# Second and third attention: float32r halves of two heads side by side on TensorE, queries in halves, maxima ahead

## The reference

```python
def _L1_attn_ref(x, wq, bq, wk, bk, wv, bv):
    xq = (x @ wq + bq).reshape(B, S, 32, 16)
    xk = (x @ wk + bk).reshape(B, S, 8, 16)
    xv = (x @ wv + bv).reshape(B, S, 8, 16)
    q, k = _rope(xq, cos, sin), _rope(xk, cos, sin)
    k, v = repeat(k, 4), repeat(xv, 4)
    probs = softmax(einsum('bqhd,bkhd->bhqk', q, k) / sqrt(16))
    return einsum('bhqk,bkhd->bqhd', probs, v)
def _L2_attn_ref(x, w_q, w_k, w_v, w_o):
    q, k, v = proj(w_q), proj(w_k), proj(w_v)
    attn = softmax(einsum('bqhd,bkhd->bhqk', q, k) / sqrt(16))
    return einsum('bhqk,bkhd->bqhd', attn, v) @ w_o.T
```

## Time and profile before

| | us |
|---|---|
| median of 3 runs (2819.14 to 2826.78) | 2824.91 |
| profiled execution | 2823.69 |
| its span, first to last instruction | 2821.9 |

### The profile page before, as it was taken

The page is one execution under the profiler, slowest core; times in us unless marked ns, Lnnn a source line. Parts: engine busy times, 40 slices in busy tenths (PEclk is TensorE's granted clock), DMA queues, the critical chain, the costliest instruction groups (busy, mean ns, idle before and its releaser), DMA issues. The chain is left out here.

```text
span 2821.9 us, 36229 instructions
## 1 busy us (share of the span) xinstructions
PE 2376.8 (84%) x12928; PEld 1296.4 (46%) x12928; DVE 1475.5 (52%) x2491; ACT 1247.3 (44%) x1599; POOL 640.1 (23%) x478
## 2 busy tenths in 40 slices
PE   4979999999997776599999957599989996999657
PEld 3657777777776532223333223233333333444434
DVE  3564545554542545678777554287778723112253
ACT  3536565555653322065656632136655662000331
POOL 1645656565651124000000022100000001001021
PEclk8989999999998887699999968799999998999778
DMA  4861111111103111100000002401021003000001
GB/s 112 247 186 42 41 56 52 56 45 56 52 27 106 42 51 53 49 14 16 15 15 15 1 15 75 113 14 24 23 44 25 1 16 120 0 0 0 17 4 53
DMA packets 76898, 133.98 MB, mean 47 GB/s; under 512 B 29848, under 2 KB 39320, under 8 KB 74480
## 3 DMA queue, kind: packets, MB, share of 16 engines
q1 hardware_dynamic: 76784, 132.35, 15.7%
HBM read 94.44 MB, written 37.62 MB: 47 GB/s over the span
## 5 line engine op out<-in xcount | busy, mean ns | idle before, releaser
L2151 POOL TENSOR_TENSOR l0a_p_low<-yT,l0a_p_high 128x1024 fp32r<-128x1024 f32 (+7 forms) x256 | 386.1, 1536 | 281.9 <-ACT l0a_p_high L2179 281.9
L1432 DVE TENSOR_REDUCE l2a_mx<-ps 128x1 f32<-128x512 f32 x512 | 338.1, 689 | 125.6 <-PE ps L1273 124.2
L1432 DVE TENSOR_REDUCE l1a_mx<-ps 128x1 f32<-128x512 f32 x512 | 336.9, 688 | 112.2 <-PE ps L1273 110.3
L2212 DVE TENSOR_REDUCE l0a_mx<-ps 128x1 f32<-128x512 f32 (+3 forms) x384 | 203.5, 554 | 236.1 <-PE ps L2058 145.7
L1399 ACT ACTIVATE l2a_prob<-ps 128x1024 f32<-128x1024 f32 x256 | 250.5, 1019 | 131.3 <-PE ps L1312 93.7
L1399 ACT ACTIVATE l1a_prob<-ps 128x1024 f32<-128x1024 f32 x256 | 250.6, 1019 | 129.9 <-PE ps L1312 93.7
L173 POOL TENSOR_TENSOR applied<-prepared,neghalf 128x2 f32<-128x2 f32 x64 | 58.4, 913 | 900.0 <-DVE prepared L154 900.0
L1273 PE MATMUL ps<-l1a_k,l1a_q 96*128 96x512 bf16 x512 | 199.0, 398 | 64.6 <-DMA l1a_k<-l1a_k_parts 47.7
L2168 ACT ACTIVATE yT<-ps 128x1024 f32<-128x1024 f32 (+7 forms) x256 | 166.4, 650 | 186.9 <-PE ps L2080 122.9
L1273 PE MATMUL ps<-l2a_k,l2a_q 96*128 96x512 bf16 x512 | 192.0, 389 | 47.2 <-DMA l2a_k<-l2a_k_parts 34.4
L2179 ACT CAST l0a_p_high<-yT 128x1024 fp32r<-128x1024 f32 (+7 forms) x256 | 172.6, 674 | 7.1
(11 more groups left out here) (303 smaller groups left out, 4357.3 us busy)
## 6 DMA issues: line engine op xcount, KB each, us to landing
l0a_q<-l0a_q SPq DMA_DIRECT2D x32, 512.0 KB, 3.3
l0q_woh<-in_l0a_wo SPq DMA_DIRECT2D x16, 512.0 KB, 5.6
l0a_q<-f SPq DMA_DIRECT2D x32, 256.0 KB, 4.7
l0a_q<-l0q_q_pe SPq DMA_DIRECT2D x32, 256.0 KB, 3.6
l0a_recip_rows<-l0a_recip_row SPq DMA_DIRECT2D x32, 256.0 KB, 3.4
l0a_o<-l0a_o_pair SPq DMA_DIRECT2D x16, 512.0 KB, 2.8
yT<-l0a_o SPq DMA_DIRECT2D x16, 512.0 KB, 3.3
l0q_wqnT<-in_l0a_wqnT SPq DMA_DIRECT2D x16, 192.0 KB, 3.5
```

What stands on the lines that cost most here:

```text
L1432: nc.vector.tensor_reduce(mx[:, m // NT, m % NT, c:c + 1], MB[c], AX.X, ALU.max).then_inc((s_red0, s_red1)[c], 1)
L2151: nc.gpsimd.tensor_tensor(p_low[:, j % 4, P * j:T], prob[:, j % 4, P * j:T], p_high[:, j % 4, P * j:T], ALU.subtract).then_inc(s_pl, 1)
L2212: nc.vector.tensor_reduce(mx[:, qt, c:c + 1], bank(par, n)[:, 0:width], AX.X, ALU.max).then_inc(s_red, 1)
```

## The change

In `split_qk` each tile has two parts instead of three: ACT casts to float32r (`high`), DVE subtracts (`low`), and both are stored as 4-byte words in DRAM arrays of 32 rows.

In `attend` two heads lie side by side in the rows: rows 0 to 47 hold (high, low, high) of the one head's queries against (high, high, low) of its keys, rows 64 to 111 those of the other, and rows 48 and 112 the maxima against ones. One call therefore makes a pair of matmuls, one for each head, into two PSUM banks. A step is one pair of scores: two heads, 128 keys, 512 queries; a group has 32 steps in two halves of the queries. One pair of maxima is issued in each step, eight steps further ahead than one group, and the chunks use three banks in a ring, which a group's transposed maxima (now once per group) enter too. The products with the values are four matmuls of 512 queries, eight in a half, at the steps `PV_STEP`, read from `vext` without the copy to `vst`. `prob` has four slots of j. The loops of PE, ACT and DVE are written out.

```diff
-Q_RUNS = [(0, 3), (1, 2), (2, 1)]
-K_RUNS = [(0, 3), (0, 2), (0, 1)]
+STEPS = HALVES * NT * 2
+PAIRS_OF_MAX = 2 * NT * 2
+RING = 3
+MAX_ROW = 3 * HD
+AHEAD = 8
+TURN_STEP = STEPS - AHEAD + 2
+PV_STEP = (7, 8, 9, 10, 12, 14, 16, 18)
+OUT_STEP, TURN_OUT_STEP, FINISH_STEP = 19, 20, 21
...
-                    nc.scalar.copy(part[0:M, n % 2, 0, :], tile_of(n)).then_inc(s_part, 1)
-                    act.wait_ge(s_lo, 2 * n + 1)
-                    nc.scalar.copy(part[0:M, n % 2, 1, :], rest[0:M, n % 2, :]).then_inc(s_part, 1)
+                    wait_stored(act, n)
+                    nc.scalar.copy(high[0:M, n % 2, :], tile_of(n)).then_inc(s_high, 1)
...
-                    nc.vector.tensor_tensor(part[0:M, n % 2, 2, :], rest[0:M, n % 2, :], part[0:M, n % 2, 1, :],
-                                            ALU.subtract).then_inc(s_lo, 1)
+                    nc.vector.tensor_tensor(low[0:M, n % 2, :], tile_of(n), high[0:M, n % 2, :],
+                                            ALU.subtract).then_inc(s_low, 1)
...
+            def load(g):
+                s, slot = loaded[g % SLOTS][0], g % SLOTS
+                for hf in range(2):
+                    heads = slice(g * GROUP + hf, (g + 1) * GROUP, 2)
+                    sp.dma_start(q_bits[64 * hf:64 * hf + 2 * HD, slot, :, :], q_dram[:, heads, :]).then_inc(s, 16)
...
+            sp.wait_ge(s_one, b_one + 2)
+            for g in range(SLOTS):
+                load(g)
...
+            for hf in range(2):
+                nc.gpsimd.memset(k_bits[64 * hf + 32:64 * hf + 64, :, :, :], 1.0).then_inc(s_one, 1)
...
+            def max_pair(m):
...
+                for hf in range(2):
+                    wait_bank(pe, ("chunk", 2 * m + hf))
+                for hf in range(2):
+                    rows = slice(64 * hf, 64 * hf + MAX_ROW)
+                    mm = nc.tensor.matmul(bank(("chunk", 2 * m + hf)), q[rows, slot, p, qt * P:(qt + 1) * P],
+                                          k[rows, slot, p % KP, 512 * c:512 * c + 512], start=True, stop=True)
+                mm.then_inc(s_mm, 1)
...
+            def pv(g, half, j):
...
+                for hh in range(GROUP):
+                    mm = nc.tensor.matmul(O[32 * hh:32 * hh + 32, :], vext[:, j, g * GROUP + hh if OWN_KEYS else g, :],
+                                          prob[:, j % 4, hh, :], start=j == 0, stop=j == NT - 1)
+                mm.then_inc(s_pv, 1)
...
+            for m in max_at[-1]:
+                max_pair(m)
+                if m % 4 == 3 and m < PAIRS_OF_MAX:
+                    v_product(m // 4)
...
+            for at in range(TOTAL):
+                pe.wait_ge(s_exp, b_exp + at + 1)
+                if at + 2 < TOTAL:
+                    scores(at + 2)
+                for m in max_at.get(at, []):
+                    max_pair(m)
...
+                used = (HALVES * g + half) * NT + j - 3
+                if p == 0 and used > 0:
+
+                    act.wait_ge(s_pv, b_pv + used)
```

More of the change, by code:

```diff
@@ L1001, in split_qk @@
     tiles = [(u, i) for u, unit in enumerate(units) for i in range(len(unit[2]))]
[L1002 removed]
+    s_mm, b_mm = chip.shared("sa_qk", len(tiles))
+    s_high, b_high = chip.shared("sa_qk_high", len(tiles))
+    s_low, b_low = chip.shared("sa_qk_low", len(tiles))
+    stores = [chip.shared(f"sa_qk_stored{i}", 32 * (len(tiles) // 2)) for i in range(2)]
     def loads(sp):
@@ L1200, in kh @@
-    def kh(hh):
-        return hh if KH == GROUP else 0
+    q = sb("q", [P, SLOTS, 2, T], F32R)
+    k = sb("k", [P, SLOTS, KP, T], F32R)
+    q_bits, k_bits = q[:].bitcast(F32), k[:].bitcast(F32)
+    prob = sb("prob", [P, 4, GROUP, SPAN])
+    osb = sb("osb", [P, SPAN])
+    mx = sb("mx", [P, 2, 2, 2, NT, 2])
+    mcol = sb("mcol", [P, 4 * NT])
+    mrow = sb("mrow", [4 * NT, P], F32R)
+    rden = sb("rden", [P, NT // 2, GROUP])
+    LOADS = 16 * 8
+    loaded = [chip.shared(f"sa_heads_loaded{i}", LOADS * len(range(i, GROUPS, SLOTS))) for i in range(SLOTS)]
@@ new lines, in attend, with bank, wait_bank, place @@
+    ring_of = {job: r for r, job in enumerate(ring)}
+    def bank(job):
+        return ps[:, 4 + ring_of[job] % RING, :]
+    def wait_bank(engine, job):
+        r = ring_of[job] - RING
+        if r < 0:
+            return
+        kind, n = ring[r]
+        if kind == "chunk":
+            engine.wait_ge(s_red, b_red + n + 1)
+        else:
+            engine.wait_ge(s_mrow, b_mrow + n + 1)
+    def place(m):
+        g, i = divmod(m, PAIRS_OF_MAX)
+        p, rest = divmod(i, NT * 2)
+        return g, p, rest // 2, rest % 2
@@ new lines, in max_turn, with v_product @@
+            def max_turn(g):
+                pe.wait_ge(s_neg, b_neg + g + 1)
+                wait_bank(pe, ("turn", g))
+                nc.tensor.transpose(bank(("turn", g))[0:4 * NT, 0:P], mcol[:], chip.ident[:]).then_inc(s_mt, 1)
+            def v_product(t):
+                if t >= 4:
+                    pe.wait_ge(s_vout, b_vout + t - 3)
+                for c in range(KC):
+                    mm = nc.tensor.matmul(ps[:, t % 4, 0:NV], chip.yT[:, c, t * P:(t + 1) * P], wv[:, c, :],
+                                          start=c == 0, stop=c == KC - 1)
+                mm.then_inc(s_v, 1)
@@ new lines, in scores @@
+            def scores(at):
+                g, half, j, p = step_of(at)
+                slot = g % SLOTS
+                if at % STEPS == 0:
+                    s, b = placed[g % 2]
+                    pe.wait_ge(s, b + 32 * (g // 2 + 1))
+                for hf in range(2):
+                    rows = slice(64 * hf, 64 * hf + EXT)
+                    mm = nc.tensor.matmul(ST[at % 2][:, hf, :], k[rows, slot, p % KP, j * P:(j + 1) * P],
+                                          q[rows, slot, p, SPAN * half:SPAN * half + SPAN], start=True, stop=True)
+                mm.then_inc(s_st, 1)
```

458 lines of the change are left out of this document (186 added, 272 removed).

## The result

The changed kernel takes **2959.98 us** (median of 4 runs, 2953.68 to 2964.54) where the kernel before takes 2825.0: ratio 1.048, 95% interval 1.0454 to 1.0506. Slower; the forecast was 2795, its range 2725 to 2862.

The account below looks back on a forecast made before the run. PE was taken to set the steady step. Second attention -12 + 7 + 25 - 39 = -19 us, third -1 + 10.5 + 20 - 39 = -9.5, against 2823.7 gave 2795 us, range 2725 to 2862.

Parts of the forecast that it names:

- clock high in the steady part: Assumption of the forecast for both attentions' steady parts: PE stays at high clock, a group takes 51.2 us against 56.0.
- rival A: The forecast itself: pairs overlap, clock high in the steady part; 2795 us, range 2770 to 2820, chance 0.40.
- B: Rival: the clock falls between the products in the steady parts, a third of low time lost; 2840 us, chance 0.23.
- stall of step 8: Once in each half, PE waits for the exponential that waited for step 7's values: 1.10 us.
- the thin steps 3 to 6: Four steps in a row in which PE streams only about 0.22 x 2 of each 1.26 us; B's place for low clock.
- PE's bunch of four products is dense: Argument against B: four of a half's eight products with the values stand in consecutive steps 7 to 10.
- plain step: Steady step without values: the next pair waits for a reduction, 1.26 us.
- the step with values: Steady step set by PE: scores 0.33, maxima 0.22, change over 0.11, values 1.00, together 1.66 us.
- the last 40 steps: End of each attention's steady part, without maxima beside the steps: 18.7 us a half, 47 us in all.
- Side by side: Two heads' matmuls of a pair run at once in different rows: 0.22 us a pair, 0.44 if one after the other.
- Ahead of the first step: First chunk to first scores, 80 chunks instead of 64: +25 us in the second attention, +20 in the third.
- Loads and split: First group's loads wait for memsets: +7 us second attention, +10.5 third; split of tiles saves 12 and 1 us.

Follow-up runs that it names:

- t1_stall: together_1 with the first two products with the values of each half at steps 7, 8 instead of 6, 7: 2859.4 us, ratio 1.0112.
- first_at_6: Changed kernel with one number changed: first product with the values of each half at step 6 instead of 7; 2852.18 us, ratio 1.0103.
- values_early: Changed kernel with products with the values at steps 6, 7, 9, 11, 12, 14, 16, 18, half's end one step earlier: 2833.6 to 2916.6 us.
- t1_no_fill: together_1 without the extra pairs of scores in steps 4 and 5: 2793.8 us, ratio 0.9899.
- together_1: Changed kernel with v_quarters, values_early, scores issued four times in steps 4 and 5, and ones cleared slot by slot: 2770.8 us, ratio 0.9816.
- serial_pairs: Changed kernel with both matmuls of each pair on the same rows, so they can't run side by side: 3562.44 us, ratio 1.263.
- v_quarters: Changed kernel with a quarter of the values' rows behind each of the first 32 pairs, not a whole product behind every fourth: 2926.31 us, ratio 1.0379.
- fill_thin: Changed kernel with the pair of scores issued three times in the steps without values: 2957.55 us.
- fill_dense: Changed kernel with the pair of scores issued three times in the steps with values: 2962.15 us.
- single_waits: Changed kernel with each chunk of a pair waiting for its own bank and signalling alone: 2875.59 us, ratio 1.0185.

## Why the prediction was wrong

The step that failed is "clock high in the steady part": rival A was taken over B, with 51.2 us for a group where 61.4 were measured. The runs show 43% and 41% of the two steady parts at 1.2 GHz in its place, and a stall of step 8 that cost 2.6 to 3.5 us instead of 1.10.

- **The clock.** B had the mechanism and a share too small: it took 15% or a quarter of the time as low (its bound, the whole), and it was 43% (204 of 475 us) and 41%. Its price, a third of the low time, was about right. Taken from t1_stall, 2.5 us for 6.8 low ones, 23.9 low us of a group would cost 8.8 us; what is left of 61.4 by first_at_6's 51.0 and two stalls of 1.45 is 7.5, or 0.31 us for each low one. At that rate the two steady parts lost an estimated 64 and 60 us, 124 of the 165 by which the forecast missed. first_at_6 itself gives 0.41 (56.6 us in a group with 13.7 low against 51.0), so the share of the clock may be larger.
- **Where it falls.** B looked at the thin steps 3 to 6 and did not count the stall behind them, and the forecast set the stall down at its own 1.10 us. Without it (first_at_6) low time falls by 117 us in each attention, and the steady parts by 56.6: 16 stalls of 1.45 are 23, the rest, 33, is clock and the fourth product of the bunch. So the wait cost up to 3.5 us each and not 1.1; under the fill (t1_stall) it cost 2.6. The thin steps do their part, as B said: in one half of each group the clock falls among them, ahead of the stall; values_early and t1_no_fill have no such stall and still groups with 27.3 us low and 61.4 in all; and the extra matmuls of together_1 take low to 24 and 19 us. The stall makes low clock more likely and longer, but it is not needed for it. The argument against B, "PE's bunch of four products is dense", did not hold: the bunch itself ran at 1.2 GHz in part (the half shown first) or whole, since the clock had fallen ahead of it. On the timeline of the kernel after, two of its steps, 3.01 us apart:

```profile
1324.48 0.63 PE L1301 MATMUL ps<-l1a_k,l1a_q 48*128 48x512 f32 x2
1325.04 1.93 PE L1341 MATMUL ps<-l1a_prob,l1a_vext 128*32 128x512 f32 x8
...
1327.49 0.63 PE L1301 MATMUL ps<-l1a_k,l1a_q 48*128 48x512 f32 x2
```

  What the chip goes by is open: serial_pairs stayed low with PE busy 96%, first_at_6 stood at 2.4 GHz in halves with PE busy 19.97 of 25.36 us, and the changed kernel fell to 1.2 though PE never waits longer than 1.20 us between matmuls in its steady groups.
- **Step sizes.** 1.26 for a plain step held (1338.08 - 1336.81 = 1.27); the step with values takes 1.77 instead of 1.66, because its pair comes alone behind a wait: values 0.43 after its start, not 0.33. Eight times 0.11 in a half, two halves: 1.8 us a group; forecast without stall 49.0, measured 51.0. The stall itself is 1.45 at high clock instead of 1.10. Together, with the last 40 steps, about 20 us in each attention.
- **Side by side**, taken as 0.22 us a pair: right; at high clock the next pair starts 0.23 us behind a pair, not 0.44, and the two of a pair start 3 or 4 ns apart. The Trainium skill ("TensorE: Matmul & The Clock Gate", Part 3) has it that tiles in different row groups run at once and start about 4 ns apart, and the trace agrees.
- **Ahead of the first step.** Second attention +28.4 against +25, low clock throughout as forecast, though PE was busy for 45.9 of 72 us there and not under half of the time; each group of four pairs took 7.7 us (1152.23 to 1159.97) against 7.4 (timeline):

```profile
1152.23 0.79 PE L1301 MATMUL ps<-l1a_k,l1a_q 48*128 48x512 f32 x2
...
1157.97 2.08 PE L1315 MATMUL ps<-l1a_wv,yT 128*128 128x128 f32 x8
...
1159.97 0.79 PE L1301 MATMUL ps<-l1a_k,l1a_q 48*128 48x512 f32 x2
```

  Third attention +40.6 against +20, and against +30 as the forecast's upper end: the product with 512 columns was priced at high clock, 3.4 us, and stood at both levels, 5.3 us in the row below, with DVE idle behind it (timeline of the third attention's start):

```profile
1886.96 5.38 PE L1315 MATMUL ps<-l2a_wv,yT 128*128 128x512 f32 x8
...
1892.38 0.58 ACT L1389 COPY l2a_vext<-ps 128x512 f32<-128x512 f32 x1 [43.88 <-PE ps L1315]
1892.80 1.29 DVE L1418 TENSOR_REDUCE l2a_mx<-ps 128x1 f32<-128x512 f32 x2 [4.45 <-PE ps L1301]
```

  v_quarters gives 27.8 us of it back.
- **Loads and split.** The memsets took 5.36 us in the second attention as worked out from the earlier trace rows, and the split's unit fell from 17.7 to 13.7 us (forecast -4.4). But the loads themselves got shorter, where the forecast had added 2 us for more bytes: from the first load's issue to the first chunk are 9.3 us (1127.54 to 1136.83) where there were 18.4 (1133.93 to 1152.33), and 12.4 in the third attention (1868.92 to 1881.31) where there were 24.5 (1800.97 to 1825.44). Why is open; no run takes the loads apart. Hence -11.8 + 5.4 - 9.1 = -15.5 for -5, and -1.3 for +9.5. The first load of the kernel before, then the timeline of the kernel after:

```profile
1133.93 1.96 SPq L1213 DMA_DIRECT2D l1a_q<-l1a_q_parts  x3
```

```profile
1122.15 5.36 POOL L1286 MEMSET l1a_k<- 32x3072 f32 x2 [8.11 <-POOLq L1038]
...
1127.54 0.36 SPq L1257 DMA_DIRECT2D l1a_q<-l1a_q_parts  x1
...
1136.83 0.79 PE L1301 MATMUL ps<-l1a_k,l1a_q 48*128 48x512 f32 x2 [33.94 <-DMA l1a_k<-l1a_k_parts]
```

The sum: -28.5 was forecast, +138.3 measured. Steady parts +83 and +78 more than forecast, third attention's start +21, second's +3, behind the last scores +3, loads and split -21: 167, the difference.

## What to carry to other kernels

Work that is taken off a full PE can take its clock with it: price each stretch at both levels, and count as part of a thin stretch every wait of PE behind it, since what follows may run at half the clock; here a wait of 1.2 us cost 2.6 to 3.5. Look first for the producer that one consumer waits for, and issue it one step earlier. In these runs extra matmuls paid where PE waits for another engine anyway (steps 4 and 5 here), and not where they push that engine's next work (fill_thin) or lengthen steps that PE sets (three of fill_dense's).

## What the runs showed of the hardware

- Busy with matmuls of 48 rows one after the other in the place of the pairs, TensorE stayed at 1.2 GHz for 754 us with a busy share of 96%; the changed kernel, with two side by side and 81% busy, had 2.4 GHz in 57% of its steady part.
- The clock of the changed kernel falls once in nearly every half although no gap between its matmuls is longer than 1.20 us (steady groups of both attentions).
- The two matmuls of a pair start 3 or 4 ns apart in rows 0 to 48 and 64 to 112, and 426 to 595 ns apart where both take the same rows (serial_pairs).
- The same program can take more than one course. values_early had groups of 61.4 and of 52.3 us, with 27.3 and 3.4 us of low clock, within one execution, and went from 2833.6 to 2916.6 us over four, where the kernel before stays within 0.3% of its median.
- A tenth of a us less in two steps (single_waits) went with 82 and 45 us less low clock. The kernel gained 84 us by it, where the steps alone are 0.10 x 216 = 22 us and the parts ahead of the first step 10 and 13; the remaining 39 fit 127 low us at 0.31.
